# Moving a route computation behind the first attention group, gathering whole rows, and reordering the start of the last stage

## The reference

```python
xn = layernorm(x)
s = attention(xn, wq, wk, wv, wo)        # 32 heads of 16, 8 K/V heads, rope, causal
logits = xn @ W_gate + b_gate            # 8 experts, the best 2 of each token
g = mean of relu(xn @ W_e[e] + b_e[e]) over the token's 2 experts
x = x + s * silu(g)
xn = layernorm(x)
s = causal convolution of xn with a 512-tap kernel K, computed from an S4 state, + D * xn
g = xn @ (weight * block scales).T + bias
out = x + s * silu(g)
```

## Time and profile before

| | |
|---|---|
| median of 3 runs | 689.17 us (687.06 to 692.37) |
| the profiled execution's own time | 686.85 us |
| its span, first to last instruction | 684.9 us |
| mean granted TensorE clock | 0.979 |
| busy: PE, DVE, ACT, POOL | 625.2, 551.0, 289.1, 353.5 us |

### The profile page before, as it was taken

How to read it: one execution, slowest core, us unless ns; L and a number is a source line. 1 busy time by engine, 2 the same in 40 slices (tenths; PEclk the granted TensorE clock), 3 DMA queues, 4 the chain that set the end, 5 groups by cost and what they waited for, 6 DMA issues and landing times.

```text
span 684.9 us, 12390 instructions
## 1 busy us (share of the span) xinstructions
PE 625.2 (91%) x3574; PEld 338.8 (49%) x3574; DVE 551.0 (80%) x1790; ACT 289.1 (42%) x535; POOL 353.5 (52%) x497
## 2 busy tenths in 40 slices
PE   8899998698989999999999999998998999589997
PEld 5788784243433334333433343333443333378886
DVE  6688899668977788987888788787798873869995
ACT  4443226234344344443544444434453343345441
POOL 3777541537765723466464157664335614576630
PEclk9999999769999999999999999999999999899999
DMA  7599989355667455173562635627246327567841
GB/s 260 153 332 252 337 214 178 64 79 178 102 197 122 106 89 80 39 135 88 102 109 60 88 62 118 114 83 118 52 88 117 120 71 228 107 153 206 208 127 77
DMA packets 55567, 92.67 MB, mean 135 GB/s; under 512 B 10328, under 2 KB 23320, under 8 KB 55504
## 3 DMA queue, kind: packets, MB, share of 16 engines
q1 hardware_dynamic: 41890, 66.45, 41.5%
q0 software_dynamic: 8576, 18.62, 12.7%
q10 hardware_dynamic: 5038, 6.84, 4.0%
HBM read 61.93 MB, written 29.43 MB: 133 GB/s over the span
## 4 chain that ended last, share of the span: by engine, by line
PE 61%; DVE 24%; issue 6%; POOL 3%; DMA 2%; ACT 2%; another core or an unknown queue 1%; ACTq 1%; SPq 0%; DVEq 0%; POOLq 0%
PE bank L1685 15%; DVE bank L1406 12%; PE bank L1024 8%; PE bank L1657 7%; PE bank L1604 7%; PE bank L2150 6%; PE bank L1696 4%; PE bank L2155 4%; DVE arena L1406 2%; PE bank L1630 2%; PE bank L1641 2%; DVE m_parts L1419 2%; PE bank L1683 1%; PE bank L1001 1%; DMA arena<-xn_rows,slots_i 1%
## 5 line engine op out<-in xcount | busy, mean ns | idle before, releaser
L1406 DVE CUSTOM_DVE_ANT_0 bank<-bank,cst 128x384 f32<-128x384 f32 (+3 forms) x512 | 235.0, 522 | 52.4 <-PE bank L1604 44.2
L1527 ACT ACTIVATE arena<-bank 128x512 f32<-128x512 f32 x320 | 172.8, 601 | 193.8 <-PE bank L1630 121.4
L1356 POOL DMA_INDIRECT arena<-xn_rows,slots_i x156 | 150.4, 964 | 53.7 <-issue 40.1
L1343 POOL TENSOR_SCALAR_AFFINE_SELECT arena<-arena 128x512 f32<-128x512 f32 x128 | 80.8, 646 | 174.7 <-ACT arena L1527 174.0
L1685 PE MATMUL bank<-w_e,arena 128*128 x312 | 160.7, 621 | 0.0
L1604 PE MATMUL bank<-kt,qt 48*128 48x512 f32 (+1 forms) x496 | 113.8, 344 | 6.2 <-DVE arena L1406 6.1
L1604 PEld LDWEIGHTS bank<-kt,qt 48*128 48x128 f32 x496 | 71.8, 190 | 86.7 <-DVE arena L1406 46.2
L1657 PE MATMUL bank<-arena 128*32 128x512 f32 (+3 forms) x1024 | 87.3, 449 | 10.1 <-ACT arena L1527 8.3
L1630 PE MATMUL bank<-qt,kt 50*128 50x512 f32 x256 | 90.5, 458 | 1.1 <-DMA qt<-arena 0.7
L1685 PEld LDWEIGHTS bank<-w_e,arena 128*128 128x128 f32 x312 | 53.7, 191 | 57.2 <-issue 53.6
L1406 DVE DVE_READ_ACCUMULATOR2_ANT arena<- 128x1 f32 x512 | 73.0, 143 | 0.0
(11 more groups left out here) (172 smaller groups left out, 942.3 us busy)
## 6 DMA issues: line engine op xcount, KB each, us to landing
qt<-turned_parts SPq DMA_DIRECT2D x96, 128.0 KB
turned_parts<-qk_parts SPq DMA_DIRECT2D x8, 1280.0 KB
expert_rows<-arena SPq DMA_DIRECT2D x39, 256.0 KB
w_e<-in_L_ffn_W_e ACTq DMA_DIRECT2D x24, 256.0 KB, 6.4
kt<-turned_parts SPq DMA_DIRECT2D x96, 64.0 KB, 7.3
arena<-in_L_attn_x SPq DMA_DIRECT2D x16, 256.0 KB, 6.6
xn_rows<-arena SPq DMA_DIRECT2D x16, 256.0 KB, 6.6
w_e<-in_L_attn_x SPq DMA_DIRECT2D x16, 256.0 KB
```

The costliest lines, as they stand in the source:

```text
L1343: g.affine_select(out=diag, in_=diag, compare_op=ALU.is_ge, fill=0.0, base=0, pattern=[[0, 2], [0, HALF], [1, P]], channel_multiplier=-1). ...
L1356: e.indirect_dma_start(xg[m % 2][:, n * P:(n + 1) * P], None, xn_q, bass.IndirectOffsetOnAxis(ap=slots_i[:, n, m:m + 1], axis=0)).then_inc ...
L1406: i = v.tensor_tensor_reduce(out=part, in0=part, in1=const("mask")[:, S - w:], scale=1.0, scalar=LOWEST, op0=ALU.add, op1=ALU.max, accum_o ...
L1527: nc.scalar.activation(pt[:, s, first:second + 1:second - first].rearrange("p c r q -> p c (r q)"), s2_bank(b, h, n).rearrange("p (c x) -> ...
```

## The change

Stage a to b: ACT does group 0's ten exponentials and the last turned parts first, and `act_places` after them. DVE keeps only the first product of `dve_tiles`; the other two go to POOL (`pool_tiles`) behind its first select. `dve_places` goes behind four blocks of group 1's maxima, and `dve_tokens`, `dve_rows`, `dve_experts` go to the end of `dve_a`. PE's 28 dummy matmuls go; `pe_back` goes behind all of group 0 and the first blocks of group 2's pass 1, with 12 dummy matmuls ahead of it, into bank 2; group 1's third block of pass 2, which uses that bank, waits for the tokens. `pe_tokens` and the quarter-row arithmetic go.

Gather: one indirect DMA a tile takes whole rows of 2 KB into `xr` (two tiles of `s_tok` that are free), SP stores the tile to DRAM (`gathered_rows`) and loads it again with four DMAs in the layout that `expert_x` wants. `rows_plan()` sets where each of the three steps stands, two half groups to one and a half group ahead. In SP's queue, `shuffles(b, h, 0)` stands ahead of `maximum_rows`, and `shuffles(b, h, 1)` between it and `load_stacks`.

Last stage: the index copies go; the first two `rows` come behind POOL's first select of the last group; DVE does `dve_scale`, the high parts of the weights and `prepared(0)` ahead of `finish` of the last group.

```diff
@@ rows_plan (whole)
+def rows_plan():
+    gathered, stored, loaded = {}, {}, {}
+    places = {m: (b * KV + h, slot) for (b, h, slot), tiles in TURNS.items() for m in tiles}
+    for m in range(MT):
+        g, slot = places[m - 2] if m > 1 else (0, 1)
+        q = 2 * g + 1 if slot == 0 else 2 * (g + 1)
+        loaded.setdefault(divmod(q, 2), []).append(m)
+        q -= 1
+        stored.setdefault(divmod(q, 2), []).append(m)
+        gathered.setdefault((q // 2, 0) if q > 1 and q % 2 else (max(q // 2 - 1, 0), 2), []).append(m)
+    return gathered, stored, loaded
@@ dve_a, after the last sequence
             dve_slots(e, st)
-            dve_tiles(e, st)
-            dve_places(e)
+            dve_tiles(e)
             for n in (0, 1):
                 maxima(e, 0, 1, n)
             turned_low(NB - 1, 1)
-            dve_tokens(e, st)
-            maxima(e, 0, 1, 2)
-            dve_rows(e, st)
-            maxima(e, 0, 1, 3)
+            for n in (2, 3):
+                maxima(e, 0, 1, n)
+            dve_places(e)
             turned_low(NB - 1, 2)
...
             maxima_rows(e, 0, 1)
-            dve_experts(e, st)
             for n in (0, 1):
                 maxima(e, 0, 2, n)
+            dve_tokens(e, st)
+            dve_rows(e)
+            dve_experts(e, st)
@@ act_a, at its end
-            act_places(e)
             for n in range(4):
                 exps(e, 0, 0, n)
...
-            maximum_rows(e, 0, 1, 1)
+            act_places(e)
@@ pe_a, at its end
-            keep_awake(28, bank[0])
-            pe_back(e)
             scores(e, (2, 3), (0, 1), (2, 3), (0, 0))
...
             scores(e, (0, 1), (0, 2), (), None)
+            pe_back(e)
@@ pe_back, pool_tiles
+            e.wait_ge(b_e, NJ)
+            keep_awake(12, bank[2])
             e.wait_ge(r_tile, 1)
+        def pool_tiles(e):
+            e.wait_ge(r_equal, 1)
...
+            g.tensor_tensor(of_tile[:, :, 1, :], of_tile[:, :, 0, :], number_b..., ALU.mult).then_inc(r_number, 1)
+            e.wait_ge(r_number, 1)
+            alone(e)
+            g.tensor_scalar(of_tile[:, :, 0, :], of_tile[:, :, 0, :], const("part"), None, ALU.mult).then_inc(r_tile, 1)
@@ gather
                 if m > 1:
-                    e.wait_ge(m_xt, m - 1)
+                    e.wait_ge(m_xs[m % 2], 16 * (m // 2))
...
-                for n in of_quarters:
-                    e.indirect_dma_start(xg[m % 2][:, n * P:(n + 1) * P], None, xn_q, ...)
+                e.indirect_dma_start(xr[m % 2], None, xn_d, ...slots_i[:, m:m + 1]...).then_inc(m_x[m % 2], 16)
@@ pool_b, the last group
                     select(b, h, 0)
+                    if (b, h) == (0, 0):
+                        pool_tiles(e)
                     next_gather(b, h, 0)
+                    if (b, h) == (NB - 1, NG - 1):
+                        for u in range(2):
+                            rows(e, 0, u)
                     select(b, h, 2)
                     if (b, h) == (NB - 1, NG - 1):
-                        rows(e, 0, 0)
+                        more_rows(e, 0, 0)
@@ dve_b, the last group
                         dve_tap_parts(e)
+                        dve_scale(e)
                         dve_taps(e, st)
+                        dve_scaled_high(e)
+                        prepared(e, st, 0)
                         finish(b, h)
-                        dve_scale(e)
@@ scores_2
+            if (b, h, n) == (0, 1, 2):
+                e.wait_ge(r_tokens, 1)
@@ sp_b
+            def shuffles(b, h, place):
+                for m in LOADED.get((b * NG + h, place), ()):
+                    e.wait_ge(m_xs[m % 2], 16 * (m // 2 + 1))
+                    if m > 1:
+                        e.wait_ge(m_xt, m - 1)
...
+                    for c in range(KB):
+                        e.dma_start(xg[m % 2][32 * c:32 * (c + 1), :]..., rows[c]).then_inc(m_xl[m % 2], 16)
+                for m in STORED.get((b * NG + h, place), ()):
+                    e.wait_ge(m_x[m % 2], 16 * (m // 2 + 1))
+                    e.dma_start(x_rows[m], xr[m % 2]).then_inc(m_xs[m % 2], 16)
@@ sp_b, go
                     stores(b, h, 0, 1)
+                    shuffles(b, h, 0)
                     if b * NG + h + 1 < NB * NG:
                         maximum_rows(e, *next_group(b, h, 1), 0)
+                    if (b, h) == (0, 0):
+                        maximum_rows(e, 0, 1, 1)
+                    shuffles(b, h, 1)
                     stores(b, h, 2)
                     if h % 2 and b * NG + h + 3 < NB * NG:
                         load_stacks(e, *next_group(b, h, 3))
@@ rows
-            nc.gpsimd.tensor_copy(c_slot[:, u], slots[:, :, bass.ds(b * TPB + u, 1)]).then_inc(c_idx, 1)
-            e.wait_ge(c_idx, b * TPB + u + 1)
@@ dve_c, its start
-            e.wait_ge(b_s, TPB)
-            prepared(0)
-            dve_scaled_parts(e)
             shift(0, 0)
-            prepared(1)
+            dve_scaled_low(e)
+            prepared(e, st, 1)
```

More of the change, by code:

```diff
@@ L99 @@
 TURNS = turns()
[L102 to L117, removed]
+def rows_plan():
[9 more added lines that the diff above has]
+    return gathered, stored, loaded
+GATHERED, STORED, LOADED = rows_plan()
 COLS = {}
@@ L1214, in build @@
         OT_END = used[0]
+        xr = [s_tok[:, NB - 1, u] for u in (2, 3)]
         xg = [take([P, D])]
@@ L1920, in inverse_root @@
                 g.tensor_tensor(c_rstd[:, u, :], c_mv[:, u, 1:2], const("half"), ALU.pow).then_inc(c_root[u % 2], 1)
-            rows(e, 0, 1)
-            for u in range(2):
-                more_rows(e, 0, u)
+            more_rows(e, 0, 1)
             rows(e, 0, 2)
             inverse_root(0, 0)
+            rows(e, 0, 3)
             more_rows(e, 0, 2)
-            rows(e, 0, 3)
             inverse_root(0, 1)
@@ L1994, in guarded, with prepared, dve_scale, dve_scaled_high @@
                 v.tensor_scalar(c_mv[:, u, 1:2], c_mv[:, u, 1:2], EPS, None, ALU.add).then_inc(c_stat[u % 2], 1)
+            return gated, layer_in, statistics, moments, guarded
+        def prepared(e, st, u):
+            gated, layer_in, statistics, moments, guarded = dve_inputs(e, st)
+            if u == 0:
+                e.wait_ge(b_s, TPB)
+            gated(0, u)
+            layer_in(0, u)
+            statistics(0, u)
+            moments(0, u)
+            guarded(0, u)
+        def dve_scale(e):
+            v = nc.vector
+            e.wait_ge(c_w, 48)
+            w4 = w_lin.rearrange("p k (o c) -> p k o c", o=KB)
+            sc4 = c_scale.rearrange("p o k -> p k o").unsqueeze(3)
+            for k in range(KB):
+                i = v.tensor_tensor(w4[:, k], w4[:, k], sc4[:, k].to_broadcast([P, KB, P]), ALU.mult)
+                i.then_inc(c_ws, 1)
+        def dve_scaled_high(e):
+            v = nc.vector
+            for par in range(2):
+                e.wait_ge(m_st[par], 16 * ((MT + 1 - par) // 2))
+            for k in range(KB):
+                e.wait_ge(c_ws, k + 1)
+                v.tensor_copy(w_high[:, k], w_lin[:, k]).then_inc(c_ws, 1)
+        def dve_scaled_low(e):
+            v = nc.vector
+            for k in range(KB):
+                e.wait_ge(c_ws, KB + k + 1)
+                v.tensor_tensor(w_low[:, k], w_lin[:, k], w_high[:, k].bitcast(F32), ALU.subtract).then_inc(c_ws, 1)
+        def dve_c(e, st):
+            v = nc.vector
+            gated, layer_in, statistics, moments, guarded = dve_inputs(e, st)
             def shift(b, u):
@@ L2072, in dve_c @@
             low(0, 0)
-            prepared(2)
+            prepared(e, st, 2)
             shift(0, 2)
```

121 lines of the change are left out of this document (41 added, 80 removed).

## The result

| | before | changed |
|---|---|---|
| median of the runs, us | 688.12 (686.65 to 692.37, 4 runs) | 703.67 (700.6 to 708.2, 4 runs) |
| profiled execution, us (span) | 686.85 (684.9) | 700.87 (699.1) |
| PE clock, mean | 0.979 | 0.962 |
| bytes moved by DMA, MB | 92.67 | 113.12 |

The ratio is 1.0232, 95% interval 1.0191 to 1.0273: slower by 1.9 to 2.7%, and above the range of the prediction. Some executions are slow as a whole and are left out of the ratios, so a ratio need not be the quotient of the medians.

A forecast was written before the change was run, and what follows sets the result against it. It took PE's matmuls alternating with DVE's maxima as the bound (61% and 24% of the chain). Handover 0, groups +2.7 and last stage -4.2 gave -1.5 us: 687.7 us from a median of 689.17, range 680 to 697.

The forecast's parts named there:

- B: Groups of stage b: fewer POOL gathers save DVE waits, later stacks cost PE; +2.7 us in sum.
- together 8 ... I keep 5 of the 8: Odd groups: row loads delay the stacks in SP's queue, 8 us in nine or ten groups, 5 kept after DVE's catching up.
- A: Handover from stage a to b: no gain or loss, 0 us, between -1.5 and +3.
- C: Last stage: earlier row fetches and fewer POOL copies save 4.2 us, between -5.5 and -1.5.
- A wait of some 0.5: SP's queue, place 1 loads: wait of some 0.5 us where the tile's own place 0 store goes out late.
- DVE's wait for rows: Groups: DVE's 2.7 us of waiting for gathered rows goes, -1.8 us on the path.
- Rival 2: SP's queue in odd groups: stacks late, nothing caught up, price 12 us; in sum +7.7, 696.9 us; chance 0.15.
- Selects behind gathers that wait for a store: ... nothing: POOL in the groups: the store was issued half a group before, so selects behind such gathers cost nothing.
- T: Handover: the end of `pe_back` on PE, 131.2 at full clock, 134 at half, taken as 132.
- rival 3: Handover: `pe_back` at half clock and long hops make tile 0 3.5 us late; +1.5 in sum, 690.7 us; chance 0.15.
- The sum in which they block DVE's places: Handover: by the shared-port rule a POOL product blocks DVE's places up to 2.8 us, making the sum 2.5 us longer.
- rival 4: Last stage: DVE waiting in front of `finish` limits the gain to -1.5; +1.2 in sum, 690.4 us; chance 0.1.

The follow-up runs named there:

- e7: Changed kernel with dummy matmuls in PE's waits for the stacks in eight groups; 1.0111 of before, 698.71 us.
- n1_before: The kernel before, unedited, profiled on a chip where before takes 674.13 us; one run, 676.09 us.
- e1: Changed kernel with the twelve stack DMAs ahead of the place 1 row loads in SP's queue; 1.0125 of before, 682.87 us.
- n4: e12 unedited, run again beside e14 on one chip; 0.9869 of before, 679.89 us.
- e12: e1 plus tile 2's gather behind group 1's first select, weights' low parts ahead of prepared(0), four row buffers from tile 12; 0.9847 of before, 679.85 us.
- e14: e12 with the old handover in place of the new one; 0.9824 of before, 676.77 us.
- e6: e1 with the handover undone, as in the kernel before; 1.0008 of before, 675.45 us.
- e10: Kernel before with the last-stage change, weights' low parts ahead of prepared(0), POOL's first add behind selects 3 and 1; 0.9969 of before, 687.24 us.

## Why the prediction was wrong

**The step that failed is B's term "together 8 ... I keep 5 of the 8".** The three parts came out at +1.8 (A), +13.4 (B) and -1.0 us (C), by the lag at `turn_maxima` of groups 2 and 31 and at the end, against 0, +2.7 and -4.2. B's mechanism, queue and groups were right, and the mean delay too: by the two timelines of the record, the first stack DMA is later against `turn_maxima` by 0.7 to 4.0 us in eleven groups, 2.2 on average, inside "1.9 to 2.8". Three things made 8 too small.
- The slack. I took off 0.3 to 1.5 us a group, and 0.5 for gathers that no longer share the engines. In the trace PE waits about what the stacks are delayed (for group 8 they go out 3.6 us later, and PE waits 3.73): in all 22.5 us, with next to nothing to take off.
- The store. "A wait of some 0.5" was 2.66 us in group 6. The load in place 1 follows its store of place 0 by less than the store needs to land.
- The clock, which I had counted in the handover and not here. Of the trace's seven longest waits for stacks (1.75 to 3.73 us) six were followed by a lower clock, 1.7 us of lost work each and 3.3 in group 8; e7's medians give 8 to 11 us back.

22.5 and about 12 are 34; the lag of the groups is 13.4 (from +1.8 to +15.2), so more than half was caught up or given back, as I had argued. Part of what was given back are the late copies of the maxima, ten of them behind quarter gathers in the trace of before. This gain I had not seen: I had read the collision in L1419, not in L1429. Where before does not pay it (n1_before), the same edit costs twice as much. B's smaller terms were off as well: DVE's wait for rows did not go (2.5 us for 2.7, forecast -1.8), and L1419's 15.0 us fell to 11.2, under the forecast 12 to 18.

**Rival 2** named the outcome: slower, SP's queue, "nothing caught up". Its condition (a mean delay of 2.8 with a slack under 1) was close; its price of 12 us had no clock in it. I gave it 0.15, and the forecast 0.35, on a slack that only one pair of rows showed.

**"Selects behind gathers that wait for a store: ... nothing"** failed too. POOL waits 55.6 us for stores. Most of it PE does not wait for, but at group 1 it idles 2.92 us, and in e1 10.2 us in 7 places.

**A** had T right (PE ended `pe_back` at 132.8, at full clock in its dummies; forecast 132), and the first turn of tile 0 at 145.3, inside 141.5 to 146. Its price was +1.8 us at group 2 in the record, inside its bounds; but it is 3.1 us between the medians of n4 (e12 again) and e14 on one chip, and 7 to 8 between e1 and e6 on two. The hole behind tile 2's gather and the late first tiles, which is rival 3's place, are the part that the traces show. POOL's two products took 2.28 and 5.55 us where I had at most 2.8 each; the cover held. The sum in which they block DVE's places did not come about: these took 2.290 us beside the second product and 2.282 before. But they had started 0.09 us ahead of it, so the case that I had priced, POOL first, did not occur, and whether the product's 5.55 us hold a wait for them is not shown.

**C** alone came out at -4.3 for -4.2, with some luck, since its own stage shows 2.5 us of that in the traces, and it was wrong in the changed kernel: -1.0. The rows landed 8.6 us after their issue, not 4.3 to 4.8, behind 2 MB of weights and x that SP had issued from 580 to 584. DVE waited 4.6 us ahead of `finish`, the place of rival 4. PE's first tile came at 611.8, less the lag 596.6, as before (596.2) and not at 593.2.

## What to carry to other kernels

A DMA that is put into a queue costs every DMA behind it its issue time and its waits. Ask which of those is awaited last, put that one first, and take slack off only where more than one row shows it. Price an idle stretch of PE with the clock that follows it: filling the holes with dummies gave about half of the loss back, by the medians, and closing one hole only moved PE to the next, longer one (e10). And compare two kernels on more than one chip: here the loss was 2.3% on one, 2.7% on a second and 4.5% on a third.

## What the hardware showed that I had not expected

- The kernel before takes 688 to 691 us in four sets of runs and 674 to 676 in two, while the changed kernel, without quarter gathers, takes about the same beside both (704.6 beside 674; 703.7 and 708.0 beside 688 and 691). In the traces of before, 0.4 us of phase between POOL and DVE goes with 1.2 us at a copy.
- A wait of 2.40 us was followed by a clock of 1.00, one of 2.35 us by 0.77.
- On POOL a 128x1248 bf16 operation with two inputs took 2.28 us, on DVE 1.46. One with one input took 5.55 and 0.56; on POOL it never ran without DVE's places beside its first 2.2 us, so how much of the 5.55 is its own is not shown.
